# Gated graph network on one core: states turned by VectorE and device memory instead of TensorE

## The reference

```python
adj_norm = adj / (jnp.sum(adj, axis=-1, keepdims=True) + EPS)
h = concat([x, adj_norm @ x]) @ weight + bias
x = layernorm(x + relu(h))

A = (adj != 0)
h = x
for l in range(5):
    m = h @ weight[l]
    agg = einsum('bij,bid->bjd', A, m)
    gi, gh = agg @ w_ih.T + b_ih, h @ w_hh.T + b_hh
    r, z = sigmoid(i_r + h_r), sigmoid(i_z + h_z)
    n = tanh(i_n + r * h_n)
    h = (1 - z) * n + z * h
out = layernorm(x + h * mask)
```

## Time and profile before

| what | value |
|---|---|
| median of 3 runs | 625.32 us (624.67 to 625.62) |
| the profiled execution | 624.76 us, its span 623.0 us |
| PE busy | 604.4 us |
| DVE, ACT, POOL busy | 515.1, 411.3, 366.5 us |
| granted TensorE clock | 0.995 of full speed |
| a steady window | 36.97 us |

### The profile page before, as it was taken

One profiled execution on the slowest core, in us unless ns is written; L12 is line 12 of the kernel. 1 busy time (PEld: TensorE's weight loads), 2 busy tenths in 40 slices (PEclk: granted clock), 3 DMA queues, 4 the chain that ended last, 5 costly groups with the idle time before them and its releaser, 6 DMA issues.

```text
span 623.0 us, 10141 instructions
## 1 busy us (share of the span) xinstructions
PE 604.4 (97%) x2877; PEld 492.6 (79%) x2877; DVE 515.1 (83%) x1177; ACT 411.3 (66%) x777; POOL 366.5 (59%) x299
## 2 busy tenths in 40 slices
PE   6999999999999999999999999999999999999993
PEld 5677888888888888888888888888888888887772
DVE  5987978897988879798897979889798887967677
ACT  4866776858667585766758576685866758564551
POOL 0644555757666575765658576576766657555343
PEclk9999999999999999999999999999999999999997
DMA  8531222231232323223231331333124131010101
GB/s 270 213 102 68 101 69 102 99 104 52 84 134 68 101 68 121 80 84 114 88 101 51 99 120 67 118 100 102 51 84 135 67 101 34 17 34 1 51 1 52
DMA packets 48080, 54.63 MB, mean 88 GB/s; under 512 B 2880, under 2 KB 27968, under 8 KB 48064
## 3 DMA queue, kind: packets, MB, share of 16 engines
q1 hardware_dynamic: 47792, 54.31, 26.3%
q10 hardware_dynamic: 272, 0.13, 0.1%
HBM read 46.57 MB, written 7.86 MB: 87 GB/s over the span
## 4 chain that ended last, share of the span: by engine, by line
PE 91%; DVE 4%; DMA 1%; ACT 1%; issue 1%; SPq 1%; POOL 0%; POOLq 0%; DVEq 0%
PE ps_tok L1292 12%; PE ps_tok L1299 12%; PE ps_r L1157 6%; PE ps_r L1158 6%; PE ps_r L1159 6%; PE ps_z L1159 6%; PE ps_z L1158 6%; PE ps_z L1157 6%; PE ps_tok L1152 5%; PE ps_b L1157 3%; PE ps_b L1158 3%; PE ps_b L1159 3%; PE ps_in L1157 3%; PE ps_hn L1159 3%; PE ps_in L1158 3%; PE ps_in L1159 3%
## 5 line engine op out<-in xcount | busy, mean ns | idle before, releaser
L594 POOL TENSOR_TENSOR h_lo<-h,h_hi 128x512 fp32r<-128x512 f32 x64 | 82.9, 1295 | 107.5 <-ACT h_hi L624 107.5
L604 POOL TENSOR_TENSOR z_h<-z_gate,h 128x512 f32<-128x512 f32 x80 | 110.0, 1374 | 43.1 <-ACT z_gate L801 43.1
L624 ACT ACTIVATE tok_hi<-ps_tok 128x512 fp32r<-128x512 f32 x63 | 37.7, 598 | 96.2 <-PE ps_tok L1152 96.2
L1292 PE MATMUL ps_tok<-edges,tok_hi 128*128 (+1 forms) x320 | 87.9, 397 | 0.7 <-ACT tok_hi L624 0.7
L1136 DVE SCALAR_TENSOR_TENSOR r_hn<-ps_hn,gru_bias,r_gate 128x512 f32<-128x512 f32 x80 | 59.9, 748 | 34.5 <-ACT r_gate L791 33.4
L1299 PE MATMUL ps_tok<-edges,tok_lo 128*128 (+1 forms) x320 | 87.7, 396 | 0.0
L724 ACT ACTIVATE ps_in<-ps_in,gru_bias 128x512 f32<-128x512 f32 x80 | 52.8, 660 | 52.8 <-DVE ps_in L1020 52.7
L544 POOL TENSOR_TENSOR adjt_lo<-adjt_in,adjt_hi 128x512 fp32r<-128x512 f32 x56 | 71.8, 1302 | 4.2 <-ACT adjt_hi L624 4.2
L1292 PEld LDWEIGHTS ps_tok<-edges,tok_hi 128*128 128x128 f32 x320 | 59.8, 188 | 15.4 <-ACT tok_hi L624 0.9
L1299 PEld LDWEIGHTS ps_tok<-edges,tok_lo 128*128 128x128 f32 x320 | 59.9, 188 | 14.8 <-DVE tok_lo L827 0.3
L827 DVE TENSOR_TENSOR tok_lo<-ps_tok,tok_hi 128x512 fp32r<-128x512 f32 x63 | 43.6, 692 | 27.9 <-ACT tok_hi L624 27.9
(11 more groups left out here) (146 smaller groups left out, 1574.2 us busy)
## 6 DMA issues: line engine op xcount, KB each, us to landing
adjt_in<-in_adj_t_dram SPq DMA_DIRECT2D x14, 1024.0 KB, 5.3
adj_in<-in_adj_dram SPq DMA_DIRECT2D x14, 1024.0 KB, 5.4
x_in<-in_x_dram SPq DMA_DIRECT2D x16, 256.0 KB, 2.8
xt_in<-in_x_t_dram SPq DMA_DIRECT2D x15, 256.0 KB, 2.6
out_dram<-y_out SPq DMA_DIRECT2D x15, 256.0 KB, 2.3
passage<-last_blocks SPq DMA_DIRECT2D x14, 256.0 KB, 2.0
last_rows<-passage SPq DMA_DIRECT2D x56, 64.0 KB, 2.0
adjt_in<-in_adj_t_dram SPq DMA_DIRECT2D x4, 256.0 KB, 4.6
```

What stands on the lines that cost most here:

```text
L594: nc.gpsimd.tensor_tensor(h_lo[new][:], h[new][:], raw(h_hi[new][:]), ALU.subtract).then_inc(s_h_lo, 1)
L604: nc.gpsimd.tensor_tensor(z_h[:], z_gate[:], h[own][:], ALU.mult).then_inc(s_zh, 1)
L624: return nc.scalar.activation(dst, src, ACT.Copy)
L1292: nc.tensor.matmul(ps_tok[:], tok_hi[:, c * P:(c + 1) * P], edges_from(c, unit[0]), start=c == 0, stop=False)
```

## The change

In windows 3 to 14 the states for slots 1 to 4 (`MOVED`) are turned as the last state was. DVE transposes the new state in blocks right behind `new_state` in slots 4 (for the next window's slot 1), 0, 1 and 2 (`state_blocks`); SP stores the blocks and loads the rows (`store_state`, `load_state`); one slot later ACT makes `tok_hi` out of the rows and POOL, no longer DVE, `tok_lo`. PE has no transposes in slots 0 to 3 of these windows. PE starts a moved unit's hi matmuls when `tok_hi` is there and waits for `tok_lo` only ahead of the lo matmuls. POOL's `tok_lo` stands behind `rstd1_of_batch` in slot 3 and behind rstd2 and cent2 in slot 2; the last scaling (y_out) moves from slot 2 to slot 3, behind z_h.

Further: the edges of a batch are made in two operations of 128x1024, both in slot 2, instead of four of 128x512 in slots 1 and 2. The first residual and the operations that read it use the PSUM bank `ps_b[0]` instead of the tile `pre1`. ACT's row sums write their unused full result over `r_gate` or `y_out`, each waiting for the one before. SP's order becomes: trip of slot 1's state with that of the last state, xt, trips for slots 2, 3 and 4, adjt, adj, x, out. The loop has one trip less, window 14 being written out.

```diff
+MOVED = {slot: UNITS[slot][1] for slot in (1, 2, 3, 4)}
+def is_moved(batches, n, slot):
+    return 3 <= n < batches - 1 and slot in MOVED
...
+        if self.next_moved(slot):
+            return None
         after = (self, slot + 1) if slot + 1 < SLOTS else (Window(self.batches, self.first + 1, self.trip), 0)
...
+    def starts_trip(self, slot):
+        if slot == SLOTS - 1:
+            return is_moved(self.batches, self.first + 1, 1)
+        return slot in (0, 1, 2) and self.trips()
...
             def window(w):
+                b = w.batch(-2) if w.loads() else None
+                if w.trips():
+                    store_state(w, 2)
                 if w.moves():
-                    move_last_state(w)
+                    store_blocks(last_blocks, passage, s_blocks, w.finished(1, 1), s_passed)
+                if w.trips():
+                    load_state(w, 2)
+                if w.moves():
+                    load_rows(last_rows, passage, s_passed, w.finished(16, 16), s_rows)
                 if w.loads():
                     sp.wait_ge(s_xt_lo, w.prepared(1, 1))
                     load_xt(b)
+                if w.trips():
+                    store_state(w, 4)
+                    load_state(w, 4)
+                    store_state(w, 1)
+                    load_state(w, 1)
+                    store_state(w, 3)
+                    load_state(w, 3)
...
# POOL
                         rstd1_of_batch()
                     if w.finishes() and slot == 2 and (w.prepares() or w.idles()):
                         last_norm()
+                    if w.next_moved(slot):
+                        pool.wait_ge(s_tok_hi, w.turned(slot + 2))
+                        nc.gpsimd.tensor_tensor(tokens(tok_lo), rows_by_tokens(MOVED[slot + 1]),
+                                                tokens(raw(tok_hi[:])), ALU.subtract).then_inc(s_tok_lo, 1)
...
                         nc.gpsimd.tensor_tensor(z_h[:], z_gate[:], h[own][:], ALU.mult).then_inc(s_zh, 1)
+                    if w.finishes() and slot == 3 and w.prepares():
+                        last_scale()
...
# ACT
+                    if w.next_moved(slot):
+                        k = MOVED[slot + 1]
+                        act.wait_ge(s_state_rows[k], w.passed(Q * 16))
+                        evacuate(tokens(tok_hi), rows_by_tokens(k)).then_inc(s_tok_hi, 1)
...
# DVE
+                def edge_half(half):
+                    cs = slice(2 * half, 2 * half + 2)
+                    nc.vector.tensor_scalar(edges[:, bass.ds(ring, 1), cs, :].rearrange("p o c m -> p (o c m)"),
+                                            adj_in[:, cs, :].rearrange("p c m -> p (c m)"), 0.0, None,
+                                            ALU.not_equal).then_inc(s_edges, 2)
+                def state_blocks(slot):
+                    k = w.unit_before(slot)[1] + 1
+                    dve.wait_ge(s_h, w.units(slot))
+                    if slot in (1, 2):
+                        dve.wait_ge(s_state_passed[4 if slot == 1 else 1], w.passed(16))
+                    nc.vector.transpose(blocks[k][:].rearrange("p q c j -> p c q j"),
+                                        h[w.home_made(slot)][:].rearrange("p (c q j) -> p c q j", c=C, q=Q)
+                                        ).then_inc(s_state_blocks[k], 1)
...
                         if slot == 2 and not w.ramps():
-                            edges_of((2,))
+                            if w.first >= 3:
+                                dve.wait_ge(s_agg, w.last_layers())
+                            edge_half(0)
...
+                    if w.starts_trip(slot):
+                        state_blocks(slot)
...
                             mean_parts(w)
                             if not w.ramps():
-                                edges_of((3,))
+                                edge_half(1)
...
-                            if not w.ramps():
-                                if w.first >= 3:
-                                    dve.wait_ge(s_agg, w.last_layers())
-                                edges_of((0, 1))
...
+            def first_residual(w):
+                return pre1[:] if w.ramps() else ps_b[0][:].rearrange("p (c d) -> p c d", c=C)
```

More of the change, by code:

```diff
@@ L118, in next_turned, with next_moved, trips, passed @@
         return after if unit and unit[1] > 0 else None
+    def next_moved(self, slot):
+        return slot + 1 < SLOTS and is_moved(self.batches, self.first, slot + 1)
+    def trips(self):
+        return is_moved(self.batches, self.first, 1)
+    def starts_trip(self, slot):
+        if slot == SLOTS - 1:
+            return is_moved(self.batches, self.first + 1, 1)
+        return slot in (0, 1, 2) and self.trips()
+    def passed(self, each, ahead=0):
+        return self.value(lambda n: each * (n - 2 + ahead))
     def end_slot(self):
@@ L178, in turned, with turned_here @@
         return self.units(slot, range(1, LAYERS))
+    def turned_here(self, slot):
+        return self.value(lambda n: count(self.batches, n, slot, range(1, LAYERS), True))
     def until_made(self, slot, layers=range(LAYERS)):
@@ L309, in program @@
         last_rows = sb("last_rows", [P, Q, C, SQ])
+        early_blocks = sb("early_blocks", [P, Q, C, SQ])
+        late_blocks = sb("late_blocks", [P, Q, C, SQ])
+        blocks = {4: early_blocks, 1: early_blocks, 3: early_blocks, 2: late_blocks}
+        passages = {k: nc.dram_tensor(f"passage{k}", [P, N], F32, kind="Internal").ap() for k in range(1, LAYERS)}
+        rows = {k: sb(f"rows{k}", [P, Q, C, SQ]) for k in range(1, LAYERS)}
         ps_tok = bank("ps_tok")
@@ L390, in program @@
         s_last = sem("s_last")
+        s_state_blocks = {k: sem(f"s_state_blocks{k}") for k in range(1, LAYERS)}
+        s_state_passed = {k: sem(f"s_state_passed{k}") for k in range(1, LAYERS)}
+        s_state_rows = {k: sem(f"s_state_rows{k}") for k in range(1, LAYERS)}
         s_blocks = sem("s_blocks")
@@ L409, in all_windows @@
                 window(Window(B, n))
-            with eng.Fori(0, B - 4) as trip:
+            with eng.Fori(0, B - 5) as trip:
                 window(Window(B, 3, trip))
-            for n in range(B - 1, B + 3):
+            for n in range(B - 2, B + 3):
                 window(Window(B, n))
@@ L630, in y_hi_of, with row_sum_of @@
                          ps_b[half][:].rearrange("p (c k d) -> p c k d", c=2, k=2)[:, :, 1, :]).then_inc(s_y_hi, 1)
-            def row_sum_of(c, of):
-                nc.scalar.activation(sum_of[:, c, :], of[:, c, :], ACT.Copy,
+            def row_sum_of(c, of, earlier):
+                if earlier is not None:
+                    act.wait_ge(s_row_sum, earlier)
+                scratch = y_out[:].rearrange("p c d -> p (c d)") if of is second_adj or earlier is None and c == 0 else r_gate[:]
+                nc.scalar.activation(scratch, of[:, c, :], ACT.Copy,
                                      accum_out=row_sum[:, c:c + 1]).then_inc(s_row_sum, 1)
@@ L790, in window @@
                             act.wait_ge(s_rhn, w.units(slot))
+                        if slot == 1 and w.prepares() and w.first > 0:
+                            act.wait_ge(s_row_sum, w.prepared(C, C))
                         nc.scalar.activation(r_gate[:], ps_r[:], ACT.Sigmoid, bias=rz_bias[:, 0:1]).then_inc(s_r, 1)
@@ L1286, in window @@
                         else:
-                            pe.wait_ge(s_tok_hi if w.leads() else s_tok_lo, w.turned(slot + 1))
+                            parted = w.leads() or is_moved(B, w.first, slot)
+                            pe.wait_ge(s_tok_hi if parted else s_tok_lo, w.turned(slot + 1))
                         for c in range(C):
```

86 lines of the change are left out of this document (50 added, 36 removed).

## The result

The changed kernel takes 621.57 us (median; 620.73 to 623.56), the kernel before 624.54 us beside it (623.97 to 625.62): ratio 0.9952, 95% interval 0.9944 to 0.9961, 3.0 us faster. The profiled execution took 621.62 us, its span 619.5 us. One slow execution is left out of what follows, 650.55 us at a mean granted clock of 0.977, of the kernel in the last experiment.

The account below looks back on a forecast made before the run. PE, busy for the whole 36.97 us window, was taken as the bound: 36.97 - 1.76 + 1.62 = 36.83 us, 12 x 0.14 = 1.7 us gained, 623.1, by the median 623.6 us. Own range 618 to 630; with rivals 610 to 631.

Parts of the forecast that it names:

- What leaves PE: Four state transposes ahead of each of slots 1 to 4, 0.44 us per group: 21.1 us at most.
- The wait: PE waits for POOL's tok_lo in slot 4, including agg_lo's 0.6 us in slot 3: 1.62 us per window.
- (a) DVE: Four block transposes per window replace four tok_lo on DVE: 1 us of work in all, counted as nothing.
- (c) ACT: tok_hi read from SBUF instead of PSUM, and row sums waiting for one another, 0.15 us x 4 in slot 1: nothing.
- (e) SP: adjt's load moves to about 2 us into slot 3; both loads in by about 11, next block store about 12.5.
- (b) The trip: States go through device memory, about 5.4 us after the blocks; hidden, with slot 1's having the least time.
- (d) The residual in PSUM: Its readers in slot 3 change by at most 0.1 us; norm1 in slot 4 has DVE time over: nothing.
- (f) POOL: Four tok_lo of 1.29 us per window, 62 us more, to about 29 us of a 35 us window.
- The bound of -5 us: In slot 2, rstd2 not held up longer puts h_lo at 4.8 to 6.05 and r_hn at 0.16: -5 us.
- Rival 1: Slot 2's edge half gets in before POOL's h_lo, so PE waits only 0.69 us: 612.5 us; chance 0.30.
- Rival 2: POOL is no bound, full 21.1 us gained: 604.2 us; needs var 0.7 us earlier still; chance 0.07.
- Rival 3: The trip of slot 1's state lands 2 us late, costing about 1 us per window: about 636 us; chance 0.15.

Follow-up runs that it names:

- the last experiment: The mended kernel with SP issuing the adjt and adj loads ahead of the trip of slot 4's state: 637.74 to 641.17 us, ratio 1.0236.
- the mended kernel: The changed kernel with POOL's tok_lo ahead of rstd1 in slot 3 and the second edge half in slot 0: 606.10 us, ratio 0.9712.
- The two moved orders: The changed kernel with only POOL's tok_lo ahead of rstd1 in slot 3: 612.33 us; with only the second edge half in slot 0: 611.16 us.

## Why the prediction was right, and where not

**What leaves PE** (21.1 us, 1.76 per window): right. Slots 0 to 2 lost 0.46, 0.46 and 0.44 us, and the mended kernel's window is 35.20 us. The full gain of 604.2 came out as 606.1, mostly because PE still waits in the first two windows of the loop.

**The wait** (1.62 us per window): 1.53. Step by step, predicted and measured: h_lo from 5.2 to 6.5 us into slot 2, 5.20 to 6.50; edge half due at 5.5, 5.77; its end 7.15, 7.05; r_hn 0.6 us into slot 3, 0.50; tok_lo's matmuls at 8.58 us with 0.11 for the restart, 8.37 without it. The edge half came up 0.27 us later than predicted, which cost nothing, as it had to wait for h_lo's end anyway. The two moved orders show that both places are causes and not only neighbours: either edit alone takes the part of the wait that the chain gives to it. Sum: 36.83 against 36.70 us, 1.7 against 3.1 us of gain, 623.6 against 621.57 us. Of the 2.0 us between, 1.5 are the 0.13 us per window (623.1 against a profiled 621.62), mostly the 0.1 us by which r_hn came sooner; the other 0.5 is the 0.56 us that I added for a median above the profiled execution, which the changed kernel doesn't have.

**(a) DVE, (c) ACT, (e) SP:** nothing, as forecast; with the chain mended the steady window has PE busy throughout, with all three in it. The place of slot 4's block transpose isn't nothing, though: it stands in slot 2 ahead of the edge half, and the prediction has it in that chain. adjt was issued 2.5 us into slot 3 (about 2 forecast), the loads were in by about 10.4 (11), the next store of blocks came at 12.3 (12.5). The edges' form belongs here: 621.83 against 621.57 us.

**(b) The trip** is hidden: tok_hi for slot 4 starts 3.74 us into slot 3 (about 4.0 forecast), with 0.48 us of wait. Slot 1's, which had the least time, starts 3.79 us into slot 0 (3.8 forecast), without a wait. The legs took 2.0 us each, not the 2.6 of the formula that the prediction put beside them. The Trainium skill ("DMA: Bandwidth & Descriptors", Anatomy of one DMA) has that formula for DMAs that GpSimd issues; SP issues these.

**(d) The residual in PSUM, "nothing":** the step that failed. The sum held by luck, because norm1 takes 1.36 us after and took 1.43 before, beside a single z_h, as DVE's and POOL's timelines of the kernel before have it:

```profile
361.45 1.43 DVE L931 TENSOR_SCALAR x<-pre,mv,rstd 128x128 f32<-128x128 f32 x4
```

```profile
360.73 1.29 POOL L604 TENSOR_TENSOR z_h<-z_gate,h 128x512 f32<-128x512 f32 x1 [0.36 <-ACT z_gate L801]
```

But the same change puts tok_lo ahead of that z_h and y_out behind it, and from SBUF norm1 then takes 3.29 us. The edit is worth 8.5 us to the changed kernel. The term was put at nothing because DVE has time over in slot 4; it has less than the 1.9 us that norm1 would have taken longer. I had costed it against the kernel before, not against POOL's new row of instructions in slot 4, though I had used for exactly such a meeting in slot 2.

**(f) POOL:** 48 tok_lo of 1.294 us are 62.1 us, a window holds 29.2 of it, both as forecast. It was the order that cost, not the 29 us.

**The bound of -5 us** (rstd2 not held up, h_lo at 4.8): out of reach. With rstd2 at 1.01 us h_lo started at 5.0 and waited for h_hi; 2.4 us came of it.

**Rival 1** (612.5): its condition didn't hold in the changed kernel, as the edge half came up 0.57 us behind h_lo. Its number is about right for the nearest kernel, 611.16 us with the edge half taken away from h_lo. **Rival 2:** its bar was var 0.7 us sooner than in rival 1, and no run got var that early. The way to the full window was to take tok_lo out from behind rstd1, and to move the edge half for agg_lo's sake. **Rival 3** (636): slot 1's trip was in time. With slot 4's made late by force, such a delay is shown to cost time; what the rival's price left out is the clock, which added 1.7 us to the window shown.

## What to carry to other kernels

Where a step moves to a less loaded engine, the free time says little: look for what stands ahead of it in that engine's order and when that is released, and put it ahead of whatever hangs on a longer chain (9 us here for an exchange of two instructions behind 4.3 us of idle time). Then go through POOL's new unbroken stretches and ask which TENSOR_SCALAR operations of DVE from SBUF come up inside them: in these traces each waited for the end of the POOL instruction that ran. Moving such an operation to a slot where nothing hangs on it takes away the price (it met POOL there too, and took 1.70 us); an operand in PSUM takes away the meeting.

## What the runs showed of the hardware that was not expected

- A series of short DVE operations from SBUF against POOL instructions without a gap is let through one at a time: 4 x 342 ns became 3.29 us. The prediction knew of one operation held up once.
- Not every one-input operation of DVE is held up. In the changed kernel a TENSOR_SCALAR of 128x4 took 0.94 us beside h_lo in slot 1 instead of 0.17, but the block transposes of 128x512 from SBUF took 0.71 us in the middle of POOL instructions, as long as before.
- The meeting is symmetric: the edge half 0.15 us ahead of h_lo holds it up by 0.44 us (1.74 instead of 1.30).
- The tok_lo waits of 0.65 us shown, twelve of them, left the granted clock at 1.00; so did six idle stretches of up to 1.51 us with the loads ahead. Behind each of five from 1.90 to 3.20 us the clock came down to the lower level for part of the next 4 us; the one of 1.90 cost nearly its own length again.
